# Six transformer layers on one core: the feed-forward statistics, their root and their transposes are put elsewhere in the turn

## The chip, the cores and the metric

The kernel runs on 1 core of one Trainium2 chip. The metric is the device time of one execution in microseconds (us); before the change it is 4221.26 us, the median of 3 runs (4219.84 to 4221.34). All arithmetic is float32, but for a mask of bfloat16.

## The reference, cut to what matters

The input is 8 sequences of 512 tokens with 128 features. The result is the sum of the input, one attention block over the layer-normalised input, and a stack of six layers over the same layer-normalised input. The stack is the part that matters here:

```
for i in range(6):
    x = attn_layer(shift_tokens(x), Wqkv[i], q_scale[i], k_scale[i], Wo[i]) + x
    x = ffn_layer(shift_tokens(x), ln_g[i], ln_b[i], W1[i], b1[i], W2[i], b2[i]) + x
```

- `shift_tokens` moves the upper 64 features one token down.
- `attn_layer`: 16 heads of 64. q and k are divided by their norms over the 64 features of a head, scaled and rotated; each token attends to its own window of 32 tokens and the window before it; softmax, product with v, output product `@ Wo`.
- `ffn_layer`: layer norm over the 128 features (mean, variance, `1/sqrt(var + 1e-5)`), a product with W1 to two halves of 341, `a * gelu(gate)`, a product with W2.

## The kernel before, in words

One stage (0 to about 965 us) does the first attention block; the change does not touch its code, except for one more memset ahead of it. The rest, about 3255 us, is the six layers. It is one software pipeline of **turns**, `layers` (L344) calling `turn(s)` on each engine. A turn is a block of 128 tokens; a batch (one sequence) has four turns, c = 0, 1, 2, 3, and a layer 8 batches, so there are 192 turns. Batches 2 to 6 of a layer run in a hardware loop, where semaphore values are computed from loop registers. Every engine has its own program, in the order in which the code is written, and waits on semaphores for the others. Nothing plans or reorders the work beyond that: the order in `turn` of each engine is the schedule.

In turn t several blocks are in flight at different depths (`s.has(k)`: the block k turns ahead). What each engine does in one turn, in its order, with the line numbers of the profile:

- **VectorE (DVE)**: sums of the exponentials `den` (L956) after ScalarE's exponentials, reciprocal (L958), four rotation products of q and k from PSUM (L909, L911), sums of squares `ss` for the 32 norms of a block (L968), their floor (L970) and the bit-trick guess of the root `rn` (L972); in turn 0 the **feed-forward statistics** of the last batch, `statistics` (bn_stats L918, a memset L921, bn_aggr L923, variance plus eps L926, guess L928); the residual add `x` (L979), the 32x32 transposes of the weights `pT` (L983), in turns 0, 2 and 3 the gate product of the feed-forward (L935), in turn 1 its residual add (L991), row maxima (L1002) and their subtraction (L1005) from the score PSUM, and last `qn`, the product of the rotated q and k with the root (L1012).
- **GpSimd (POOL)**: normalised weights `pn` (L630), two additions that finish the rotations of q (L634) and k (L636), then `newton`, 12 dependent small operations (L399) on 32 columns that refine the root `rn`; in turn 0 after that a second `newton` of 12 on 4 columns (`frn`), and the two products that normalise the tokens of the feed-forward, `fnt` (shown as tile xnT: L645 subtracts the mean, L649 multiplies with the root).
- **TensorE (PE)**: 16 transposes of `qn` (L1053; q to banks 0 and 1, k to banks 4 and 5), the output product (L1265, 32 matmul records into bank 0, over even and then odd heads), feed-forward work (turn 0: up product of chunk 2, L1221; turn 1: 4 transposes of `fnt` to bank 6, L1213, and the down product, L1231; turns 2 and 3: up products of chunks 0 and 1), one transpose of tokens (L1301), scores (L1313, L1318), the product of weights and windows (L1204), which waits for `pT`, and two projections (L1047). In four turns of a layer a `fold` of the next layer's weights stands behind the output product.
- **ScalarE (ACT)**: squares of q (L742), copy of the transposed q to `qT`, both banks in one activation (L746), squares of k (L749), two copies of the transposed k (L754, L755), in turn 1 the copy of the transposed feed-forward tokens (L765), in the others gelu (L734), copy of the transposed tokens (L771), two copies of the product with the windows to `y` (L726), exponentials `es` (L781).
- **SyncE (SP)**: DMA issues; the change moves none of them. The tokens that the statistics read (`xsh`) are loaded at the end of turn 3 (L543 to L545).

The order around the root on DVE before the change, within `turn`:

```
reduce ss -> floor -> guess rn -> [turn 0: statistics, guess frn] -> x += ps_o -> transpose pT -> ...
```

Of the kernel before, what the change touches and what calls it, by code (L numbers as in the profile page):

```python
# [87 lines left out]
def build(nc, x_in, consts, a_logit, a_bout, a_wqk, a_wv, a_wo, l_wqk, l_wv, l_wo, l_scale, l_w1, l_w2, l_small, out, xd, accd, vd):  # L88
# [8 lines left out]
    with ExitStack() as ctx:  # L97
# [43 lines left out]
        ss = sb("ss", [P, 2 * H])  # L141
        c15 = sb("c15", [P, 2 * H])
        root_const = sb("root_const", [P, len(ROOT_CONSTS), 2 * H])
        floor_const = sb("floor_const", [P, 2 * H])
        rn = sb("rn", [P, 2 * H])
        rt = sb("rt", [P, 2 * H])
# [169 lines left out]
        f_gs = sem("f_gs")  # L316
        f_rs = sem("f_rs")
# [234 lines left out]
        def _(pool):  # L552
# [4 lines left out]
            nc.gpsimd.memset(floor_const[:], NORM_FLOOR).then_inc(s_avg, 1)  # L557
            nc.gpsimd.memset(ones, 1.0).then_inc(s_avg, 1)
            pool.wait_ge(s_avg, 3 + len(ROOT_CONSTS))
# [65 lines left out]
            def turn(s):  # L625
                c, t = s.c, s.t
                if s.has(1):
                    pool.wait_ge(l_rd, t + 2)
                    past(pool, l_pT, t + 1)
                    nc.gpsimd.tensor_tensor(heads(pn[:], H), heads(es[:], H),  # L630
                                            rden[:].unsqueeze(2).to_broadcast([P, H, KEYS]), ALU.mult).then_inc(l_p, 1)
                if s.has(3):
                    pool.wait_ge(l_rq, t + 4)
                    nc.gpsimd.tensor_tensor(t1[:, 0:INNER], t1[:, 0:INNER], t2[:, 0:INNER], ALU.add).then_inc(l_rotq, 1)  # L634
                    pool.wait_ge(l_rk, t + 4)
                    nc.gpsimd.tensor_tensor(t1[:, INNER:2 * INNER], t1[:, INNER:2 * INNER], t2[:, INNER:2 * INNER],  # L636
                                            ALU.add).then_inc(l_rotk, 1)
                    pool.wait_ge(l_gs, t + 4)
                    newton(pool, l_rs, t + 3, rn[:], ss[:], rt[:], scaled=True)
                if c == 0 and s.ffn(1):  # L640
                    n = s.f1
                    pool.wait_ge(f_gs, n + 1)
                    newton(pool, f_rs, n, frn[:], fhalf[:], frt[:])
                    past(pool, f_xt, n)
                    nc.gpsimd.tensor_tensor(heads(fnt, NU), xsh[:], agg[:, :, 0:1].to_broadcast([P, NU, DIM]),  # L645
                                            ALU.subtract).then_inc(f_dv, 1)
                    pool.wait_ge(f_dv, n + 1)
                    pool.wait_ge(f_rs, (n + 1) * RS_POOL)
                    nc.gpsimd.tensor_tensor(heads(fnt, NU), heads(fnt, NU), frn[:].unsqueeze(2).to_broadcast([P, NU, DIM]),  # L649
                                            ALU.mult).then_inc(f_xn, 1)  # L650
# [5 lines left out]
        def _(act):  # L656
# [80 lines left out]
            def turn(s):  # L737
# [5 lines left out]
                if s.has(2):  # L743
                    act.wait_ge(l_tq, t + 3)
                    past(act, l_s, t + 2)
                    act.activation(qT[:].rearrange("p h c -> p (h c)"), pool0, ACT.Copy).then_inc(l_qT, 1)  # L746
# [3 lines left out]
                if s.has(2):  # L750
                    if s.turn_of(-1, 2):
                        act.wait_ge(s_zero, 2)
                    act.wait_ge(l_tk, t + 3)
                    act.activation(*keys(0, (c + 2) % NU), ACT.Copy)  # L754
                    act.activation(*keys(1, (c + 2) % NU), ACT.Copy).then_inc(l_kT, 1)  # L755
                part = fold_part(s)
# [6 lines left out]
                if c == 1 and s.ffn(1):  # L763
                    act.wait_ge(f_xt, s.f1 + 1)
                    act.activation(fxn, bank(6), ACT.Copy).then_inc(f_T, 1)  # L765
# [21 lines left out]
        def _(dve):  # L787
# [127 lines left out]
            def statistics(n):  # L915
# [6 lines left out]
                for k in range(NU):  # L922
# [3 lines left out]
                nc.vector.tensor_scalar(fhalf[:], agg[:, :, 1], EPS, 0.5, ALU.add, ALU.mult).then_inc(f_hv, 1)  # L926
                dve.wait_ge(f_hv, n + 1)
                nc.vector.tensor_scalar(frn[:].bitcast(I32), fhalf[:].bitcast(I32), -0.5, float(0x5F3759DF - (1 << 22)),  # L928
                                        ALU.mult, ALU.add).then_inc(f_gs, 1)
# [22 lines left out]
            def turn(s):  # L952
# [8 lines left out]
                if s.has(3):  # L961
                    u = (c + 3) % NU
                    dve.wait_ge(l_sqq, t + 4)
                    past(dve, l_qn, t + 3)
                    rotate(0, u, pool3, l_rq)
                    dve.wait_ge(l_sqk, t + 4)
                    rotate(1, u, pool1, l_rk)
                    nc.vector.tensor_reduce(ss[:], heads(sq[:], 2 * H), X, ALU.add).then_inc(l_ss, 1)  # L968
                    dve.wait_ge(l_ss, t + 4)
                    nc.vector.tensor_tensor(ss[:], ss[:], floor_const[:], ALU.max).then_inc(l_fl, 1)  # L970
                    dve.wait_ge(l_fl, t + 4)
                    nc.vector.tensor_scalar(rn[:].bitcast(I32), ss[:].bitcast(I32), -0.5, float(0x5F3759DF),  # L972
                                            ALU.mult, ALU.add).then_inc(l_gs, 1)
                if c == 0 and s.ffn(1):
                    statistics(s.f1)
                if s.has(0):
                    dve.wait_ge(l_o, t + 1)
                    xb = x[:, bass.ds((s.b * NU + c) * DIM, DIM)]
                    nc.vector.tensor_tensor(xb, xb, ps_o, ALU.add).then_inc(l_x, 1)  # L979
                if s.has(1):  # L980
# [26 lines left out]
                if s.has(3):  # L1007
# [5 lines left out]
                                            rn[:].unsqueeze(2).to_broadcast([P, 2 * H, DH]), ALU.mult).then_inc(l_qn, 1)  # L1013
# [3 lines left out]
            dve.wait_ge(s_avg, 3 + len(ROOT_CONSTS))  # L1017
# [4 lines left out]
        def _(pe):  # L1022
# [28 lines left out]
            def transposes(i, pool, src):  # L1051
                for a in range(PAIRS):
# [156 lines left out]
            def ffn_transpose(n):  # L1209
                pe.wait_ge(f_xn, n + 1)  # L1210
                past(pe, f_h, n * NC)
                for k in range(NU):
                    t = nc.tensor.transpose(bank(6)[:, k * P:(k + 1) * P], fnt[:, k * P:(k + 1) * P], ident)  # L1213
                t.then_inc(f_xt, 1)

# [29 lines left out]
            def turn(s):  # L1245
                c, t = s.c, s.t
                part = fold_part(s)
                if s.has(2):
# [4 lines left out]
                    transposes(0, pool0, qn[:]).then_inc(l_tq, 1)  # L1253
                    past(pe, l_y0sb, t + 1)
                    transposes(1, pool2, qn[:]).then_inc(l_tk, 1)
                if s.has(0):
                    pe.wait_ge(l_y0sb, t + 1)
                    pe.wait_ge(l_y1sb, t + 1)
                    if s.has(2):
                        pe.wait_ge(l_qT, t + 3)  # L1260
                    if s.turn_of(0, 0):
                        pe.wait_ge(s_msb, (s.l + 1) * NU)
                    for odd in range(2):
                        for h in range(odd, H, 2):
                            m = nc.tensor.matmul(ps_o, y[:, h], mhL[s.v][:, slot(h)], start=(h == 0), stop=(h == H - 1))  # L1265
                    m.then_inc(l_o, 1)
                if part is not None:
                    n, v, q = part
                    if s.has(2):
                        pe.wait_ge(l_qT, t + 3)  # L1270
                    past(pe, l_xT, t + 4)
                    fold(n, q)
                if s.turn_of(1, 1):
                    pe.wait_ge(l_qT, t + 3)
# [6 lines left out]
                if c == 1 and s.ffn(1):  # L1281
                    ffn_transpose(s.f1)
# [8 lines left out]
                if s.has(4):  # L1291
                    pe.wait_ge(l_xs[c], (s.l * NB + s.b + 2) * 16)
                    if s.has(2):
                        pe.wait_ge(l_qT, t + 3)
# [4 lines left out]
                    if s.turn_of(1, 1):  # L1299
                        pe.wait_ge(f_bs, s.l + 1)  # L1300
                    nc.tensor.transpose(ps_x[:, 0:P], xs[:, c], ident).then_inc(l_xt, 1)  # L1301
                if s.has(2):
# [6 lines left out]
                    pe.wait_ge(l_qT, t + 3)  # L1309
# [24 lines left out]
                if s.has(4):  # L1334
                    if c == 0 and s.ffn(2):
                        pe.wait_ge(f_h, (s.f2 + 1) * NC)
                    if c == 1 and s.ffn(1):
                        pe.wait_ge(f_T, s.f1 + 1)
# [104 lines left out]
```

## Time and profile before

| what | value |
|---|---|
| median of 3 runs | 4221.26 us (4219.84 to 4221.34) |
| profiled execution, its time | 4222.04 us |
| its span, first to last instruction | 4220.2 us |
| mean granted TensorE clock | 0.990 |
| busy PE, DVE, ACT, POOL | 3945.5, 3868.1, 2606.7, 2696.9 us (93, 92, 62, 64%) |
| turns of the layers | 192, in steady batches 65.09 us for four |

Busy time is an average over the span. Two engines are above 90%, so the shares alone don't say which bounds a turn; the order in time of one steady batch, and what each engine waits for in it, do. In the timeline a row is: start in us from the span's start, duration in us, engine, line, operation, output from inputs, shapes, and in brackets the idle time of that engine ahead of it with what ended it.

### The profile page before, as it was taken

The page shows a single profiled execution, that of the slowest core. Times are in us where ns is not written, and L with a number is a line of the kernel's source. Part 1 is how long each engine was busy: PE and PEld are TensorE (multiplying, and loading weights), DVE is VectorE, ACT ScalarE, POOL GpSimd, SP SyncE. Part 2 cuts the span into 40 slices and gives each one's busy share as a digit, 9 for nine tenths or more (in the row PEclk, how much of TensorE's full clock was granted, in tenths as well). Part 3 has the DMA queues.
Part 4 walks back from the last instruction along what each step waited for, and adds up shares of the span by engine and source line. Part 5 has one row for each costly group of instructions (what it writes and reads, how often), then busy time and mean ns, then how long its engine had stood idle before and what let it go on. Part 6 is the DMA issues. An engine that isn't in the chain of part 4 may idle for free. (4 is left out here: it accounts for less than half of the span.)

```text
span 4220.2 us, 124486 instructions
## 1 busy us (share of the span) xinstructions
PE 3945.5 (93%) x48616; PEld 2740.2 (65%) x48616; DVE 3868.1 (92%) x4452; ACT 2606.7 (62%) x3780; POOL 2696.9 (64%) x4716
## 2 busy tenths in 40 slices
PE   7999999997999999999999999999999999999996
PEld 5666666665666666666666666666666666666664
DVE  5888888887999999999999999999999999999994
ACT  4666666653566666666666665666666666666663
POOL 5565556645667676676667666666676666766663
PEclk9999999999999999999999999999999999999998
DMA  5454554540000011000110001100011000010000
GB/s 136 93 100 95 98 98 92 103 99 20 24 17 15 20 29 29 17 15 17 32 29 16 16 16 31 28 18 15 16 30 30 18 15 16 20 39 18 15 16 14
DMA packets 342439, 165.07 MB, mean 39 GB/s; under 512 B 114240, under 2 KB 337472, under 8 KB 341184
## 3 DMA queue, kind: packets, MB, share of 16 engines
q1 hardware_dynamic: 342208, 161.99, 17.2%
q8 instruction: 145, 2.38, 0.2%
q14 instruction: 86, 0.70, 0.1%
HBM read 115.67 MB, written 33.69 MB: 35 GB/s over the span
## 5 line engine op out<-in xcount | busy, mean ns | idle before, releaser
L630 POOL TENSOR_TENSOR pn<-es,rden 128x1024 f32<-128x1024 f32 x192 | 366.6, 1909 | 695.7 <-DVE rden L958 695.7
L726 ACT ACTIVATE y<-ps 128x1024 f32<-128x1024 f32 x384 | 372.3, 1021 | 503.8 <-PE ps L1204 503.8
L634 POOL TENSOR_TENSOR t<-t 128x1024 f32<-128x1024 f32 x192 | 454.7, 2368 | 69.0 <-DVE t L911 69.0
L678 ACT ACTIVATE t<-ps,amx 128x512 f32<-128x512 f32 x512 | 347.9, 689 | 224.5 <-DVE amx L815 224.5
L909 DVE TENSOR_TENSOR t<-ps,tabl 128x1024 f32<-128x1024 f32 x384 | 467.1, 1216 | 7.8 <-ACT sq L749 4.6
L911 DVE TENSOR_TENSOR t<-ps,tabl 128x1024 f32<-128x1024 f32 x384 | 466.4, 1215 | 0.0
L636 POOL TENSOR_TENSOR t<-t 128x1024 f32<-128x1024 f32 x192 | 453.3, 2361 | 4.7 <-DVE t L911 4.7
L1012 DVE TENSOR_TENSOR qn<-t,rn 128x2048 f32<-128x2048 f32 x192 | 438.1, 2282 | 5.0 <-POOL rn L399 5.0
L968 DVE TENSOR_REDUCE ss<-sq 128x32 f32<-128x2048 f32 x192 | 437.0, 2276 | 0.0
L1053 PEld LDWEIGHTS ps<-cst,qn 128*128 128x128 f32 x3072 | 350.2, 141 | 116.5 <-issue 64.2
L815 DVE TENSOR_REDUCE amx<-ps 128x2 f32<-128x1024 f32 x256 | 311.0, 1215 | 111.3 <-PE ps L1075 111.0
L1265 PE MATMUL ps<-acc,y 128*128 128x128 f32 x3072 | 369.9, 279 | 36.6 <-ACT qT L746 32.3
L1265 PE MATMUL ps<-wm,y 128*128 128x128 f32 x3072 | 365.7, 277 | 33.8 <-ACT qT L746 33.8
L1265 PEld LDWEIGHTS ps<-acc,y 128*128 128x128 f32 x3072 | 354.7, 194 | 57.5 <-issue 57.4
L1265 PEld LDWEIGHTS ps<-wm,y 128*128 128x128 f32 x3072 | 350.2, 192 | 53.9 <-issue 53.9
L1318 PE MATMUL ps<-kpad,qT 128*32 128x128 f32 x12288 | 383.9, 278 | 0.0
L1053 PE MATMUL ps<-cst,qn 128*128 128x128 f32 x3072 | 371.0, 274 | 13.6 <-DVE qn L1012 10.4
L1318 PEld LDWEIGHTS ps<-kpad,qT 128*32 128x32 f32 x12288 | 331.0, 111 | 44.8 <-issue 44.1
L1047 PE MATMUL ps<-wm,xT 128*128 128x512 f32 x768 | 357.5, 608 | 1.4 <-DVE acc L858 0.8
L1047 PE MATMUL ps<-acc,xT 128*128 128x512 f32 x768 | 355.2, 605 | 0.0
L823 DVE STREAM_TRANSPOSE kpad<-t 128x1024 f32<-128x1024 f32 x256 | 315.5, 1232 | 0.0
L1075 PE MATMUL ps<-qk 64*128 64x512 f32 x1024 | 289.6, 643 | 4.3 <-ACT t L678 3.5
(134 smaller groups left out, 8245.4 us busy)
## 6 DMA issues: line engine op xcount, KB each, us to landing
wm<-values_dram SPq DMA_DIRECT2D x128, 256.0 KB, 5.0
y<-values_dram SPq DMA_DIRECT2D x128, 256.0 KB, 4.7
values_dram<-qT SPq DMA_DIRECT2D x64, 256.0 KB, 2.3
tokens_dram<-x SPq DMA_DIRECT2D x96, 128.0 KB
xs<-tokens_dram SPq DMA_DIRECT2D x192, 64.0 KB, 1.8
xw<-tokens_dram SPq DMA_DIRECT2D x192, 64.0 KB, 1.9
xsh<-x SPq DMA_DIRECT2D x48, 128.0 KB
xsh<-x SPq DMA_DIRECT2D x48, 127.0 KB
```

What stands on the lines that cost most here:

```text
L630: nc.gpsimd.tensor_tensor(heads(pn[:], H), heads(es[:], H), rden[:].unsqueeze(2).to_broadcast([P, H, KEYS]), ALU.mult).then_inc(l_p, 1)
L634: nc.gpsimd.tensor_tensor(t1[:, 0:INNER], t1[:, 0:INNER], t2[:, 0:INNER], ALU.add).then_inc(l_rotq, 1)
L636: nc.gpsimd.tensor_tensor(t1[:, INNER:2 * INNER], t1[:, INNER:2 * INNER], t2[:, INNER:2 * INNER], ALU.add).then_inc(l_rotk, 1)
L726: return act.activation(y[:].rearrange("p h (w q) -> p w h q", w=NW)[:, 2 * half:2 * half + 2], src.rearrange("p (w h q) -> p w h q", w=2, ...
L909: nc.vector.tensor_tensor(t13, q3, tabl[:, 0, u, i].unsqueeze(1).to_broadcast([P, H, DH]), ALU.mult)
L911: nc.vector.tensor_tensor(t23.rearrange("p h (s d) -> p h s d", s=2), swapped, tabl[:, 1, u, i].rearrange("p (s d) -> p s d", s=2).unsquee ...
L968: nc.vector.tensor_reduce(ss[:], heads(sq[:], 2 * H), X, ALU.add).then_inc(l_ss, 1)
L1012: nc.vector.tensor_tensor(heads(qn[:], 2 * H), heads(t1, 2 * H), rn[:].unsqueeze(2).to_broadcast([P, 2 * H, DH]), ALU.mult).then_inc(l_qn, 1)
L1047: m = nc.tensor.matmul(pool[:, s * 512:(s + 1) * 512], src, wqkL[v][:, i * INNER + s * 512:i * INNER + (s + 1) * 512], start=True, stop=True)
L1053: t = nc.tensor.transpose(pool[:, a * P:(a + 1) * P], src[:, i * INNER + a * P:i * INNER + (a + 1) * P], ident)
L1265: m = nc.tensor.matmul(ps_o, y[:, h], mhL[s.v][:, slot(h)], start=(h == 0), stop=(h == H - 1))
L1318: m = nc.tensor.matmul(pool1[w * WIN:(w + 1) * WIN, a * 2 * KEYS:(a + 1) * 2 * KEYS], qT[:, a, w * WIN:(w + 1) * WIN], kpad[:, 2 * a:2 * a ...
```

## The change

- The statistics move from turn 0 to turn 1, on DVE ahead of the sums of squares. They no longer make a guess of their own. The variance plus eps goes, times the square of the norms' scale, into 4 new columns of `ss`, now 36 wide; guess, `newton` and the buffers `rn`, `rt`, `root_const` are 36 wide in every turn. `frn`, `fhalf` and `frt` are no longer used here.
- In every turn the residual add `x` stands between the sums of squares and their floor.
- POOL makes `fnt` in turn 1, after the shared `newton`.
- PE transposes `fnt` in turn 2, between the even and the odd heads of the output product, to bank 1 instead of bank 6; ACT copies it there ahead of the gelu. The feed-forward's up product of turn 2 waits for that copy as before.
- The copy of the transposed q is two activations of one bank each, each after its own 4 transposes; the output product waits for the first alone.
- DVE waits in turn 2 for `f_xn` ahead of its guess, since that overwrites the root which POOL's last product reads.

The declarations, the fill of `ss` with ones at the start, and waits whose number alone changes (`l_qT` now counts two a turn) are left out of the diff:

```diff
@@ -635,18 +634,19 @@
                                             ALU.add).then_inc(l_rotk, 1)
-                    pool.wait_ge(l_gs, t + 4)
-                    newton(pool, l_rs, t + 3, rn[:], ss[:], rt[:], scaled=True)
-                if c == 0 and s.ffn(1):
+                roots = t + 4 if s.has(3) else L * NBLK + 1 + (s.static and s.b == NB)
+                if s.has(3) or c == 1 and s.ffn(1):
+                    pool.wait_ge(l_gs, roots)
+                    newton(pool, l_rs, roots - 1, rn[:], ss[:], rt[:], scaled=True)
+                if c == 1 and s.ffn(1):
                     n = s.f1
-                    pool.wait_ge(f_gs, n + 1)
-                    newton(pool, f_rs, n, frn[:], fhalf[:], frt[:])
+                    pool.wait_ge(f_mv, n + 1)
                     past(pool, f_xt, n)
...
                     pool.wait_ge(f_dv, n + 1)
-                    pool.wait_ge(f_rs, (n + 1) * RS_POOL)
-                    nc.gpsimd.tensor_tensor(heads(fnt, NU), heads(fnt, NU), frn[:].unsqueeze(2).to_broadcast([P, NU, DIM]),
+                    pool.wait_ge(l_rs, roots * RS_POOL)
+                    nc.gpsimd.tensor_tensor(heads(fnt, NU), heads(fnt, NU), rn[:, 2 * H:].unsqueeze(2).to_broadcast([P, NU, DIM]),
                                             ALU.mult).then_inc(f_xn, 1)
@@ -741,9 +741,11 @@
                 if s.has(2):
-                    act.wait_ge(l_tq, t + 3)
                     past(act, l_s, t + 2)
-                    act.activation(qT[:].rearrange("p h c -> p (h c)"), pool0, ACT.Copy).then_inc(l_qT, 1)
+                    for half in range(2):
+                        act.wait_ge(l_tq, 2 * t + 5 + half)
+                        act.activation(qT[:, 4 * half:4 * half + 4].rearrange("p h c -> p (h c)"), bank(half),
+                                       ACT.Copy).then_inc(l_qT, 1)
                 if s.has(3):
@@ -753,6 +755,9 @@
                     act.activation(*keys(1, (c + 2) % NU), ACT.Copy).then_inc(l_kT, 1)
+                if c == 2 and s.ffn(1):
+                    act.wait_ge(f_xt, s.f1 + 1)
+                    act.activation(fxn, ps_x, ACT.Copy).then_inc(f_T, 1)
                 part = fold_part(s)
@@ -760,9 +765,6 @@
                     gelu(s.f2, 2, None)
-                if c == 1 and s.ffn(1):
-                    act.wait_ge(f_xt, s.f1 + 1)
-                    act.activation(fxn, bank(6), ACT.Copy).then_inc(f_T, 1)
                 if c >= 2 and s.ffn(1):
@@ -923,10 +925,7 @@
                 dve.wait_ge(f_mv, n + 1)
-                nc.vector.tensor_scalar(fhalf[:], agg[:, :, 1], EPS, 0.5, ALU.add, ALU.mult).then_inc(f_hv, 1)
-                dve.wait_ge(f_hv, n + 1)
-                nc.vector.tensor_scalar(frn[:].bitcast(I32), fhalf[:].bitcast(I32), -0.5, float(0x5F3759DF - (1 << 22)),
-                                        ALU.mult, ALU.add).then_inc(f_gs, 1)
+                nc.vector.tensor_scalar(ss[:, 2 * H:], agg[:, :, 1], EPS, ROOT_SCALE * ROOT_SCALE, ALU.add, ALU.mult).then_inc(f_hv, 1)

@@ -965,18 +964,25 @@
                     rotate(1, u, pool1, l_rk)
-                    nc.vector.tensor_reduce(ss[:], heads(sq[:], 2 * H), X, ALU.add).then_inc(l_ss, 1)
-                    dve.wait_ge(l_ss, t + 4)
-                    nc.vector.tensor_tensor(ss[:], ss[:], floor_const[:], ALU.max).then_inc(l_fl, 1)
-                    dve.wait_ge(l_fl, t + 4)
-                    nc.vector.tensor_scalar(rn[:].bitcast(I32), ss[:].bitcast(I32), -0.5, float(0x5F3759DF),
-                                            ALU.mult, ALU.add).then_inc(l_gs, 1)
-                if c == 0 and s.ffn(1):
+                if c == 1 and s.ffn(1):
                     statistics(s.f1)
+                if s.has(3):
+                    nc.vector.tensor_reduce(ss[:, 0:2 * H], heads(sq[:], 2 * H), X, ALU.add).then_inc(l_ss, 1)
                 if s.has(0):
...
                     nc.vector.tensor_tensor(xb, xb, ps_o, ALU.add).then_inc(l_x, 1)
+                if s.has(3):
+                    dve.wait_ge(l_ss, t + 4)
+                    nc.vector.tensor_tensor(ss[:, 0:2 * H], ss[:, 0:2 * H], floor_const[:], ALU.max).then_inc(l_fl, 1)
+                    dve.wait_ge(l_fl, t + 4)
+                if c == 1 and s.ffn(1):
+                    dve.wait_ge(f_hv, s.f1 + 1)
+                if c == 2 and s.ffn(1):
+                    dve.wait_ge(f_xn, s.f1 + 1)
+                if s.has(3) or c == 1 and s.ffn(1):
+                    nc.vector.tensor_scalar(rn[:].bitcast(I32), ss[:].bitcast(I32), -0.5, float(0x5F3759DF),
+                                            ALU.mult, ALU.add).then_inc(l_gs, 1)
                 if s.has(1):
@@ -1208,10 +1214,16 @@
                 pe.wait_ge(f_xn, n + 1)
-                past(pe, f_h, n * NC)
                 for k in range(NU):
-                    t = nc.tensor.transpose(bank(6)[:, k * P:(k + 1) * P], fnt[:, k * P:(k + 1) * P], ident)
+                    t = nc.tensor.transpose(ps_x[:, k * P:(k + 1) * P], fnt[:, k * P:(k + 1) * P], ident)
                 t.then_inc(f_xt, 1)
+
+            def tokens_transposed(s):
+
+                if s.has(2):
+                    pe.wait_ge(l_qT, 2 * s.t + 6)
+                pe.wait_ge(l_xT, s.t + 4 if s.has(4) else L * NBLK)
+                ffn_transpose(s.f1)

@@ -1250,36 +1262,41 @@
                         past(pe, l_xT, t + 4)
-                    transposes(0, pool0, qn[:]).then_inc(l_tq, 1)
+                    for half in range(2):
+                        transposes(0, pool0, qn[:], half).then_inc(l_tq, 1)
                     past(pe, l_y0sb, t + 1)
...
                     if s.has(2):
-                        pe.wait_ge(l_qT, t + 3)
+                        pe.wait_ge(l_qT, 2 * t + 5)
                     if s.turn_of(0, 0):
...
                     for odd in range(2):
+                        if odd and c == 2 and s.ffn(1):
+                            tokens_transposed(s)
                         for h in range(odd, H, 2):
...
                     m.then_inc(l_o, 1)
+                elif c == 2 and s.ffn(1):
+                    tokens_transposed(s)
                 if part is not None:
                     n, v, q = part
+                    if c == 2 and s.ffn(1):
+                        pe.wait_ge(f_T, s.f1 + 1)
                     if s.has(2):
-                        pe.wait_ge(l_qT, t + 3)
+                        pe.wait_ge(l_qT, 2 * t + 6)
                     past(pe, l_xT, t + 4)
...
                 if s.turn_of(1, 1):
-                    pe.wait_ge(l_qT, t + 3)
+                    pe.wait_ge(l_qT, 2 * t + 6)
                     ffn_bias(s.l)
...
                     ffn_up(s.f2, 2)
-                if c == 1 and s.ffn(1):
-                    ffn_transpose(s.f1)
                 if c == 1 and s.ffn(2):
@@ -1291,13 +1308,15 @@
                     if s.has(2):
-                        pe.wait_ge(l_qT, t + 3)
+                        pe.wait_ge(l_qT, 2 * t + 6)
                     past(pe, l_xT, t + 4)
...
                         pe.wait_ge(f_bs, s.l + 1)
+                    if c == 2 and s.ffn(1):
+                        pe.wait_ge(f_T, s.f1 + 1)
                     nc.tensor.transpose(ps_x[:, 0:P], xs[:, c], ident).then_inc(l_xt, 1)
@@ -1334,8 +1353,6 @@
                         pe.wait_ge(f_h, (s.f2 + 1) * NC)
-                    if c == 1 and s.ffn(1):
-                        pe.wait_ge(f_T, s.f1 + 1)
                     if c == 1 and s.ffn(2):
```

## Rows read from the trace of the kernel before

**Rows 1.** Waits between engines, 1080 to 4190 us: who waited for whom, total us, times, longest

```profile
PE ps L1204 <- DVE pT L983: 68.8, 48, 1.7
PE ps L1265 <- ACT qT L746: 64.3, 183, 0.5
PE ps L1301 <- DVE b1s L947: 14.2, 6, 4.2
...
DVE den L956 <- ACT es L781: 17.9, 89, 2.4
```

**Rows 2.** Timeline of DVE, 2400 to 2475 us: the first operation of five turns

```profile
2404.21 1.22 DVE L956 TENSOR_REDUCE den<-es 128x16 f32<-128x1024 f32 x1
...
2421.53 1.22 DVE L956 TENSOR_REDUCE den<-es 128x16 f32<-128x1024 f32 x1 [0.17 <-ACT es L781]
...
2438.34 1.22 DVE L956 TENSOR_REDUCE den<-es 128x16 f32<-128x1024 f32 x1 [0.16 <-ACT es L781]
...
2453.82 1.22 DVE L956 TENSOR_REDUCE den<-es 128x16 f32<-128x1024 f32 x1
...
2469.31 1.22 DVE L956 TENSOR_REDUCE den<-es 128x16 f32<-128x1024 f32 x1
```

**Rows 3.** Timeline of DVE, the same window: one turn 2 from its sums of squares on

```profile
2444.30 2.27 DVE L968 TENSOR_REDUCE ss<-sq 128x32 f32<-128x2048 f32 x1
2446.61 0.32 DVE L970 TENSOR_TENSOR ss<-ss,floor_const 128x32 f32<-128x32 f32 x1
2446.96 0.18 DVE L972 TENSOR_SCALAR rn<-ss 128x32 int32<-128x32 int32 x1
...
2447.30 1.24 DVE L983 STREAM_TRANSPOSE pT<-pn 128x1024 f32<-128x1024 f32 x1
...
2451.47 2.28 DVE L1012 TENSOR_TENSOR qn<-t,rn 128x2048 f32<-128x2048 f32 x1
```

**Rows 4.** Timelines of PE and of ACT, the same turn 2

```profile
2438.82 1.91 PE L1053 MATMUL ps<-cst,qn 128*128 128x128 f32 x16
...
2448.84 1.14 PE L1204 MATMUL ps<-pT,xw 32*128 32x512 f32 x8
...
2452.73 1.06 ACT L781 ACTIVATE es<-es 128x1024 f32<-128x1024 f32 x1
```

**Rows 5.** Timeline of DVE: the statistics in turn 0, the floor in turn 1

```profile
2412.96 0.87 DVE L918 BATCH_NORM_STATS2 st<-xsh 128x6 f32<-128x128 f32 x4
...
2414.28 0.17 DVE L926 TENSOR_SCALAR fhalf<-agg 128x4 f32<-128x4 f32 x1
2414.49 0.20 DVE L928 TENSOR_SCALAR frn<-fhalf 128x4 int32<-128x4 int32 x1
...
2429.80 1.20 DVE L970 TENSOR_TENSOR ss<-ss,floor_const 128x32 f32<-128x32 f32 x1
```

**Rows 6.** Timeline of POOL, 2400 to 2475 us

```profile
2414.42 0.24 POOL L399 TENSOR_TENSOR rt<-rn 128x32 f32<-128x32 f32 x1
...
2419.16 2.25 POOL L399 TENSOR_TENSOR frt<-frn 128x4 f32<-128x4 f32 x1
...
2422.21 1.05 POOL L645 TENSOR_TENSOR xnT<-xsh,agg 128x512 f32<-128x512 f32 x1
...
2428.59 2.36 POOL L636 TENSOR_TENSOR t<-t 128x1024 f32<-128x1024 f32 x1
...
2444.52 2.36 POOL L636 TENSOR_TENSOR t<-t 128x1024 f32<-128x1024 f32 x1
...
2450.83 0.25 POOL L399 TENSOR_TENSOR rn<-rn,rt 128x32 f32<-128x32 f32 x1
```

**Rows 7.** Timelines of PE and of ACT: the feed-forward tokens in turn 1

```profile
2427.83 0.60 PE L1213 MATMUL ps<-cst,xnT 128*128 128x128 f32 x4
...
2428.47 0.60 ACT L765 ACTIVATE qk<-ps 128x512 f32<-128x512 f32 x1 [1.58 <-PE ps L1213]
```

**Rows 8.** Timeline of the end of the span, PE

```profile
4196.88 4.56 PE L1231 MATMUL ps<-w,fh 128*128 128x128 f32 x24
```

More of the change, by code:

```diff
@@ L140, in build @@
         msel = sb("msel", [P, 2, P], BF16)
-        ss = sb("ss", [P, 2 * H])
+        ss = sb("ss", [P, 2 * H + NU])
         c15 = sb("c15", [P, 2 * H])
-        root_const = sb("root_const", [P, len(ROOT_CONSTS), 2 * H])
+        root_const = sb("root_const", [P, len(ROOT_CONSTS), 2 * H + NU])
         floor_const = sb("floor_const", [P, 2 * H])
-        rn = sb("rn", [P, 2 * H])
-        rt = sb("rt", [P, 2 * H])
+        rn = sb("rn", [P, 2 * H + NU])
+        rt = sb("rt", [P, 2 * H + NU])
         mx = sb("mx", [P, H])
@@ L315, in build @@
         f_hv = sem("f_hv")
-        f_gs = sem("f_gs")
-        f_rs = sem("f_rs")
         f_dv = sem("f_dv")
@@ L557, in _ @@
             nc.gpsimd.memset(floor_const[:], NORM_FLOOR).then_inc(s_avg, 1)
+            nc.gpsimd.memset(ss[:], 1.0).then_inc(s_avg, 1)
             nc.gpsimd.memset(ones, 1.0).then_inc(s_avg, 1)
-            pool.wait_ge(s_avg, 3 + len(ROOT_CONSTS))
+            pool.wait_ge(s_avg, 4 + len(ROOT_CONSTS))
             def token_root(b):
@@ L1012, in turn @@
                     nc.vector.tensor_tensor(heads(qn[:], 2 * H), heads(t1, 2 * H),
-                                            rn[:].unsqueeze(2).to_broadcast([P, 2 * H, DH]), ALU.mult).then_inc(l_qn, 1)
+                                            rn[:, 0:2 * H].unsqueeze(2).to_broadcast([P, 2 * H, DH]), ALU.mult).then_inc(l_qn, 1)
             dve.wait_ge(s_tb, 16)
             scale_tables(0)
-            dve.wait_ge(s_avg, 3 + len(ROOT_CONSTS))
+            dve.wait_ge(s_avg, 4 + len(ROOT_CONSTS))
             layers(dve, turn)
@@ L1049, in project, with transposes @@
                 return m
-            def transposes(i, pool, src):
-                for a in range(PAIRS):
+            def transposes(i, pool, src, half=None):
+                for a in range(PAIRS) if half is None else range(half * 4, half * 4 + 4):
                     t = nc.tensor.transpose(pool[:, a * P:(a + 1) * P], src[:, i * INNER + a * P:i * INNER + (a + 1) * P], ident)
@@ L1308, in turn @@
                         past(pe, l_sub, t + 2)
-                    pe.wait_ge(l_qT, t + 3)
+                    pe.wait_ge(l_qT, 2 * t + 6)
                     pe.wait_ge(l_kT, t + 3)
```

## The prediction

> **What bounds the kernel now.** The page gives PE and DVE over 90% busy, which does not say who waits for whom, so I read the waits first. PE waits for `pT` once a batch (48 times, 1.4 us each) and for the copy `qT` in nearly every turn (0.35 us each); DVE waits a little for the exponentials before `den` [rows 1]. Next, the starts of `den` give the length of each turn of a steady batch: 17.32 (turn 0), 16.81, 15.48, 15.49, together 65.10 us [rows 2]. Then I follow turn 2 on all engines. From `den` (2438.34) DVE works without a gap to the end of `pT` (2447.30 + 1.24 = 2448.54): 10.20 us [rows 2, 3]. PE starts the product with the windows 0.30 later, ScalarE copies `y` and ends `es` at 2453.79, and the next `den` starts at 2453.82 [rows 2, 4]. So there is a **ring** den, pT, windows, y, es, den of 10.20 + 5.28 = 15.48 us. PE's own order takes the same 15.48: from its transposes (2438.82) to the windows are 10.02 us, of which about 0.35 are the wait for `qT` [rows 1, 4]. In turns 2 and 3 the ring and PE are tied. In turn 0 the ring is longer by the statistics (PE waits 1.4 us at L1204), in turn 1 PE is (down product and transposes).
>
> A second thing matters: POOL and DVE block each other. In turn 2 POOL's addition L636 ends at 2446.88 and DVE's floor L970 at 2446.93; in turn 1 they end at 2430.95 and 2431.00, and there L970, a matter of 32 columns, shows 1.20 us [rows 3, 5, 6]. The other way round, a POOL operation on 4 columns that meets `qn` takes 2.25 us instead of 0.20 [rows 6]. DVE operations with both inputs in SBUF and POOL's exclude each other, and the later one waits to the other's end.
>
> **Part 1, the add before the floor (all turns).** From guess to `pT` are 0.34 us, of which the add `x` fills 0.21. The floor cannot end before POOL's addition anyway, so the add falls into that wait: the reduction's end is 2446.57, the add takes it to about 2446.8, the floor still ends at 2446.93 [rows 3, 6]. Gain on the ring between 0 (the add pushes the floor) and 0.21; I take 0.15, since waits for two semaphores now stand bare between guess and `pT`. `newton` has slack: from the guess to its last result are 4.12 us for 32 columns (2446.96 to 2451.08) and, at 1.6 ns a column and operation from the 32- and 4-column rows, 4.2 for 36. DVE needs it 4.51 - 0.21 = 4.3 us after the guess [rows 3, 6].
>
> **Part 2, the copy by banks (all turns).** PE's wait of 0.35 goes: the first 4 transposes end some 0.5 us into the 1.9, a 512-column copy takes 0.60 [rows 7], both before the k transposes end. PE's turn becomes about 15.13, the ring stays the longer one. Worth nothing by itself, but it lets Part 1 show, and pays for Part 4. It costs ScalarE some 0.1 a turn, hidden by its waits for PE.
>
> **Part 3, the statistics.** *Turn 0* loses them (1.74 with the guess [rows 5]) and follows the ring: 15.48 - 0.15 = 15.33, a gain of 1.99. POOL's own 12 small steps, the blocked one (2.25) and L645, L649 also leave turn 0, so POOL is no longer late in turn 1 and the floor is not held 0.9 us there.
> *Turn 1*, counted from `den`. The reduction used to start at 5.96 (2444.30 - 2438.34); the statistics now start there and their last operation, the `tensor_scalar` of the variance, is issued 1.32 us later, at 7.28 [rows 2, 3, 5]. POOL's L636 runs until 8.54. Does it hold that operation? At the low end it does not (reduction at 7.4); at the high end all the statistics queue behind POOL (reduction near 10.0), which their rows speak against: four bn_stats took 0.87 with POOL's small steps beside them. The nearest row is L928, also a 4-column `tensor_scalar`: 0.20 us, ending at 2414.69, 0.03 after a POOL step (2414.42 + 0.24) [rows 5, 6]. That is the pattern of L970, so I take it as held: it ends at 8.6, the reduction starts at 8.5. Then reduction, add, floor (now free of POOL) 2.7 us: guess at 11.2, `pT` from 11.33 to 12.57. By the ring the next `den` would come at 12.57 + 5.28 = 17.85. But POOL goes from `newton` (ends 11.2 + 4.2 = 15.4) without a wait into L645, 1.05 us, which reads SBUF, and DVE reaches `qn` at about 15.5: it is held until 16.45, ends near 18.6, and `den` starts at 18.55. PE is not the bound there (its 16.81 fall by 0.35 and by the transposes); it will wait for `pT` in turn 1 instead of turn 0. Turn 1: +1.74.
>
> The Trainium skill, page "SBUF — State Buffer", section "Who interferes with whom", says that a `tensor_scalar` between SBUF tensors can enter a mode with two ports and is then blocked for the whole of a GpSimd instruction, and bn_stats is not among those it names. Row L928 alone would allow a delay of 0.03 us; by the page it would be the rest of L636. The sum by the page is the one above, the sum without it is rival A.
>
> **Part 4, tokens in turn 2.** PE does the 4 transposes (0.60 alone, about 0.45 in a stream) there: PE's turn 15.13 + 0.45 = 15.6 from transposes to transposes, but after the late `qn` PE starts nearer to `den` (0.3 instead of 0.48), so 15.42 from `den` to `den`. POOL's L649 runs after `qn`, ready 1.1 us after it; PE needs it 3.7 us into its turn. ScalarE's copy (0.60) comes after its k copies, about 5.2 us into the turn, and the up product needs it at 6.0. Cost 0.09 over the ring. If the copy came 1 us later, PE would wait for it. DVE's new wait for `f_xn` was met long ago. Turn 3: 15.33. No DMA is moved.
>
> **The sum.** 15.33 + 18.55 + 15.42 + 15.33 = 64.63 against 65.10: -0.47 a batch, 48 batches: -22.6. In the six batches with the bias (PE already waits 2.4 us for DVE's `b1s` [rows 1]) turn 1 takes the 1.2 us of later statistics in full, and turn 0, which has a fold, had no 2 us to win: +1.1 each, +6.6 (estimate). At the end the down product (4.56 us [rows 8]) no longer stands between the last statistics and the last up products, the copy (0.6) and the wider root (0.6) come in: -3.3. Together -19.3 from the profiled execution, 4222.0: 4202.7. That execution is 0.8 above the median of the runs shown, well inside what I can tell. Forecast **4203 us**.
>
> **Rivals.**
> A. *The variance operation is not held by POOL.* Then in turn 1 guess at 10.1, `den` at 17.45: 63.53 a batch, -75 + 6.6 - 3.3: **4150 us**. For: L926 itself always shows 0.17 next to POOL's steps, and it reads with a step; against: it fell into a gap between two of them (2414.35 to 2414.42), and L928.
> B. *The add only pushes the floor, or the bare waits cost what it gave.* Ring 15.48, turn 2 15.55: 65.06 a batch, with the corrections **4223 us**. No change.
> C. *Slower: PE stays the bound.* The two copies, each with its fixed part and its semaphore, reach PE no earlier than one did. Then turns 0 and 3 stay 15.48, turn 2 carries the transposes (15.93), turn 1 18.55: 65.44, +16 + 3: **4241 us**. It decides from 0.35 us on, a second copy's worth. Against: the output product needs the first copy alone, and that can be done 0.6 us before the last transpose.
> D. The high end of Part 3, all statistics behind L636: turn 1 +1.4 more, **4270 us**.
>
> **Chances.** Forecast 0.57 (own range 4188 to 4217), A 0.22 (4138 to 4168), B 0.11, C 0.07, D 0.03. What a measurement of this kernel tells from no change is about 0.2%, 8 us: faster takes most of the forecast's case and all of A, 0.70; same 0.20 (B and the forecast's upper edge); slower 0.10. The range 4148 to 4226 holds the forecast, B and two thirds of A, about 0.82.
>
> **What would show it.** Turn 0 near 15.3 between two `den`, turn 1 between 17.4 and 18.6, the rest just under 15.4. PE's wait for `qT` at L1265 gone; its wait for `pT` in turn 1, about 1 us. L926 at 1.2 us instead of 0.17: the forecast; still 0.17: A. L1012 in turn 1 at about 3.2 us instead of 2.28; if it stays 2.28 in that turn the hold by L645 is wrong, and turn 1 is shorter by 0.7. `den` to `pT` unchanged in turns 2 and 3: B. L1265 starting 2.25 us after L1053 as before: C.

## The result and the profile after

The changed kernel takes 4186.18 us, the median of 4 runs (4179.85 to 4188.69), against 4220.83 us for the kernel before (4219.84 to 4221.34): ratio 0.9914, 95% interval 0.9899 to 0.993. So it is 34.7 us faster. The forecast was 4203 us, 18 us faster: right in sign, and the time lies in the range (4148 to 4226), but the kernel gained nearly twice what was forecast. The profiled execution took 4187.27 us.

The page of the changed kernel: span, then busy us and share by engine.

```profile
span 4185.5 us, 124350 instructions
...
PE 3931.9 (94%) x48616; PEld 2739.3 (65%) x48616; DVE 3844.2 (92%) x4406; ACT 2616.1 (63%) x3972; POOL 2586.2 (62%) x4165
```

The waits of PE and DVE from 1080 to 4150 us (us in total, times, longest), which answer to [rows 1]:

```profile
PE ps L1210 <- DVE pT L989: 87.1, 77, 3.5
PE ps L1320 <- DVE b1s L946: 26.4, 6, 6.2
PE ps L1059 <- DVE qn L1018: 16.2, 38, 3.2
...
DVE den L955 <- ACT es L783: 15.1, 65, 2.4
```

The wait for `qT` (64.3 us) is gone. PE now waits for `pT` and, 38 times, for `qn`: DVE has taken the lead. The wait for the bias has grown by 12 us in its six turns. Next the starts of `den` on DVE's timeline, from turn 3 of one batch to the end of turn 2 of the next, against [rows 2]:

```profile
2373.80 1.21 DVE L955 TENSOR_REDUCE den<-es 128x16 f32<-128x1024 f32 x1
...
2388.89 1.21 DVE L955 TENSOR_REDUCE den<-es 128x16 f32<-128x1024 f32 x1
...
2404.24 1.22 DVE L955 TENSOR_REDUCE den<-es 128x16 f32<-128x1024 f32 x1 [0.17 <-ACT es L783]
...
2422.59 1.21 DVE L955 TENSOR_REDUCE den<-es 128x16 f32<-128x1024 f32 x1
...
2437.67 1.21 DVE L955 TENSOR_REDUCE den<-es 128x16 f32<-128x1024 f32 x1
```

| turn | before | forecast | after |
|---|---|---|---|
| 0 | 17.32 | 15.33 | 15.35 |
| 1 | 16.81 | 18.55 | 18.35 |
| 2 | 15.48 | 15.42 | 15.08 |
| 3 | 15.49 | 15.33 | 15.09 |
| batch | 65.10 | 64.63 | 63.87 |

Turns 0 and 1 came out within 0.2 us of the forecast: turn 0 became 2.0 us shorter and turn 1 1.5 us longer. Of the miss of 0.76 us a batch, turns 2 and 3 hold 0.58 and turn 1 the rest. DVE's timeline of turn 1 and of the end of the next turn, against [rows 3, 5]:

```profile
2410.20 0.86 DVE L920 BATCH_NORM_STATS2 st<-xsh 128x6 f32<-128x128 f32 x4
...
2411.52 1.29 DVE L928 TENSOR_SCALAR ss<-agg 128x4 f32<-128x4 f32 x1
2412.72 2.27 DVE L970 TENSOR_REDUCE ss<-sq 128x32 f32<-128x2048 f32 x1
...
2415.32 0.18 DVE L984 TENSOR_SCALAR rn<-ss 128x36 int32<-128x36 int32 x1
2415.41 1.24 DVE L989 STREAM_TRANSPOSE pT<-pn 128x1024 f32<-128x1024 f32 x1
...
2419.55 3.12 DVE L1018 TENSOR_TENSOR qn<-t,rn 128x2048 f32<-128x2048 f32 x1
...
2430.93 0.24 DVE L977 TENSOR_TENSOR ss<-ss,floor_const 128x32 f32<-128x32 f32 x1
2431.20 0.18 DVE L984 TENSOR_SCALAR rn<-ss 128x36 int32<-128x36 int32 x1
2431.30 1.24 DVE L989 STREAM_TRANSPOSE pT<-pn 128x1024 f32<-128x1024 f32 x1
```

and POOL's beside it, against [rows 6]:

```profile
2410.42 2.36 POOL L635 TENSOR_TENSOR t<-t 128x1024 f32<-128x1024 f32 x1
...
2419.48 1.04 POOL L645 TENSOR_TENSOR xnT<-xsh,agg 128x512 f32<-128x512 f32 x1
2420.68 2.88 POOL L649 TENSOR_TENSOR xnT<-xnT,rn 128x512 f32<-128x512 f32 x1 [0.16 <-POOL xnT L645]
```

Both holds of the forecast are there. The `tensor_scalar` on 4 columns takes 1.29 us and ends at 2412.81, 0.03 after POOL's addition (2410.42 + 2.36 = 2412.78). `qn` takes 3.12 us, since L645 ran until 2420.52; and L649 in turn waits behind `qn` (2.88 us, against 1.04 before the change). Last PE's timeline, against [rows 4, 7]:

```profile
2399.19 1.14 PE L1210 MATMUL ps<-pT,xw 32*128 32x512 f32 x8 [0.32 <-DVE pT L989]
...
2416.78 1.14 PE L1210 MATMUL ps<-pT,xw 32*128 32x512 f32 x8 [1.65 <-DVE pT L989]
...
2422.73 1.96 PE L1059 MATMUL ps<-cst,qn 128*128 128x128 f32 x16 [0.31 <-DVE qn L1018]
2424.53 1.95 PE L1280 MATMUL ps<-wm,y 128*128 128x128 f32 x16
2426.31 0.60 PE L1218 MATMUL ps<-cst,xnT 128*128 128x128 f32 x4
2426.75 1.95 PE L1280 MATMUL ps<-wm,y 128*128 128x128 f32 x16
...
2432.67 1.14 PE L1210 MATMUL ps<-pT,xw 32*128 32x512 f32 x8
```

In turn 1 the windows start 0.13 us after `pT` (2415.41 + 1.24), although PE had stood idle, and so they do in turn 2. That is the ring's own delay there. The 0.30 between them in turn 2 of the kernel before was PE arriving. In turn 0 (the first row) the delay is 0.33 us with PE idle, in the loop's batches before and after the change alike; the cause of the difference between the turns was not tried.

### The profile page after: what moved, and what is told of

It is laid out like the page before. It is cut to its first block, busy times and chain, and to the rows that moved or that the text cites. A ratio compares the mean times of both kernels' runs of the same rounds, so it can differ in the third digit from the quotient of the medians.

```text
span 4185.5 us, 124350 instructions
## 1 busy us (share of the span) xinstructions
PE 3931.9 (94%) x48616; PEld 2739.3 (65%) x48616; DVE 3844.2 (92%) x4406; ACT 2616.1 (63%) x3972; POOL 2586.2 (62%) x4165
## 4 chain that ended last, share of the span: by engine, by line
PE 52%; DVE 25%; issue 11%; POOL 7%; ACT 4%; POOLq 0%; DMA 0%; DVEq 0%; ACTq 0%; SPq 0%
PE ps L1280 10%; PE ps L1210 7%; PE ps L1053 6%; PE ps L1337 5%; PE ps L1059 5%; PE ps L1233 5%; DVE t L911 4%; DVE qn L1018 3%; DVE t L913 3%; PE ps L1116 3%; DVE kpad L825 3%; DVE den L955 2%; POOL rt L397 2%; ACT y L726 2%; PE ps L1081 2%
## 5 line engine op out<-in xcount | busy, mean ns | idle before, releaser
L1018 DVE TENSOR_TENSOR qn<-t,rn 128x2048 f32<-128x2048 f32 x192 | 468.9, 2442 | 6.1 <-POOL rn L397 6.1
L1210 PE MATMUL ps<-pT,xw 32*128 32x512 f32 x1536 | 222.3, 648 | 95.9 <-DVE pT L989 92.0
```

What stands on the lines that cost most here:

```text
L1018: nc.vector.tensor_tensor(heads(qn[:], 2 * H), heads(t1, 2 * H), rn[:, 0:2 * H].unsqueeze(2).to_broadcast([P, 2 * H, DH]), ALU.mult).then_ ...
L1210: m = nc.tensor.matmul(pools[w // 2][:, w % 2 * 512:(w % 2 + 1) * 512], (xs if new else xw)[rows, u], pT[rows, new].rearrange("p h q -> p ...
```

## The experiments

Theory S: before the change PE alone held turns 2 and 3 at 15.48. The ring, with 0.13 in place of 0.30, was 15.31, and DVE's own order about 15.33, both just behind it. Theory R is the forecast's: the ring was 15.48 too. The change moves the statistics (the move), puts the residual add ahead of the floor (the add) and copies the transposed q by banks (the split). Kernels marked "on before" carry only the parts named; the others alter the changed kernel. "Batch" is the sum of four steady turns; in e1, e4 and e8 some batches differ, as said there. Differences in the total are between medians.

| kernel | median us | ratio to before, 95% | turns 0, 1, 2, 3 | batch |
|---|---|---|---|---|
| e1_split_alone (on before) | 4207.11 | 0.9963 (0.9951 to 0.9976) | 17.32, 16.24, 15.34, 15.33 | 64.2 |
| e2_add_alone (on before) | 4210.04 | 0.9971 (0.9961 to 0.9982) | 17.0, 16.8, 15.48, 15.48 | 64.8 |
| e8_split_and_add (on before) | 4198.07 | 0.9938 (0.9922 to 0.9955) | 18.0, 16.9, 15.1, 15.1 | 65.1 |
| e9_move_alone | 4248.06 | 1.0059 (1.0042 to 1.0076) | 15.7, 18.3, 15.6, 15.5 | 65.1 |
| e3_one_copy | 4245.44 | 1.0054 (1.0037 to 1.0071) | 15.62, 18.37, 15.62, 15.48 | 65.1 |
| e4_add_late | 4215.49 | 0.9985 (0.9975 to 0.9994) | 15.68, 18.29, 15.33, 15.33 to 15.46 | 64.6 to 64.75 |
| e5_variance_late | 4122.05 | 0.9762 (0.9746 to 0.9779) | 15.36, 17.10, 15.10, 15.1 | 62.7 |
| e6_mean_early | 4171.09 | 0.9876 (0.986 to 0.9893) | 15.35, 17.55, 15.34, 15.1 | 63.3 |
| e7_both | 4103.09 | 0.9719 (0.9703 to 0.9735) | 15.37, 16.28, 15.33, 15.1 | 62.1 |

**e1, the copy by banks alone.**

```diff
-                    transposes(0, pool0, qn[:]).then_inc(l_tq, 1)
+                    for half in range(2):
+                        transposes(0, pool0, qn[:], half).then_inc(l_tq, 1)
...
-                    act.activation(qT[:].rearrange("p h c -> p (h c)"), pool0, ACT.Copy).then_inc(l_qT, 1)
+                    for half in range(2):
+                        act.wait_ge(l_tq, 2 * t + 5 + half)
+                        act.activation(qT[:, 4 * half:4 * half + 4].rearrange("p h c -> p (h c)"), bank(half),
+                                       ACT.Copy).then_inc(l_qT, 1)
```

> The kernel before with the copy of the transposed q by banks, nothing else. Theory S (in turns 2 and 3 of the kernel before PE alone was the bound at 15.48 us, the ring over pT, windows and es had some 0.17 us of slack since pT to windows needs 0.13 us and not the 0.30 that stood there, and DVE's own order is 15.33): turns 2 and 3 fall to 15.33, turn 1 from 16.81 to about 16.5, turn 0 stays 17.3; -0.6 us a batch, about -30 us. Theory R (that of the prediction: the ring was 15.48 too): turns 0, 2 and 3 unchanged, turn 1 -0.35, about -16 us.

Measured: 15.34 and 15.33 in turns 2 and 3, as theory S had it to 0.01; R is out. DVE's timeline of one batch:

```profile
2328.18 1.21 DVE L958 TENSOR_REDUCE den<-es 128x16 f32<-128x1024 f32 x1
...
2345.50 1.22 DVE L958 TENSOR_REDUCE den<-es 128x16 f32<-128x1024 f32 x1 [0.17 <-ACT es L783]
...
2361.74 1.22 DVE L958 TENSOR_REDUCE den<-es 128x16 f32<-128x1024 f32 x1
...
2377.08 1.21 DVE L958 TENSOR_REDUCE den<-es 128x16 f32<-128x1024 f32 x1
...
2392.41 1.21 DVE L958 TENSOR_REDUCE den<-es 128x16 f32<-128x1024 f32 x1
```

The total, -15 us, missed the -30 expected. The steady batch gained 0.87, but in some ten batches turn 0 was about 1.6 us longer, and in the last layer a batch gained only 0.13. PE's row in a turn 0 of the longer kind:

```profile
3401.31 1.93 PE L1206 MATMUL ps<-pT,xw 32*128 32x512 f32 x8 [2.29 <-DVE pT L985]
```

After an idle time of 2.29 us the eight matmuls took 1.93 us and not 1.14. A PE that comes to L1206 earlier waits longer there (1.62 us before the change), and in those batches it runs slower after the wait.

**e2, the add alone.** `x += ps_o` moved from behind the guess to ahead of the floor, on the kernel before.

> The kernel before with the residual add moved ahead of the floor, nothing else. Theory S and theory R alike: PE holds turns 1, 2 and 3 at 16.81 and 15.48, so only turn 0, which PE does not hold, falls, by 0.2 to 0.25: -10 us. If instead DVE or the ring held turns 2 and 3, they fall by 0.25 each: -30 us or more.

Measured: -12 us; turn 0 -0.3, turns 1, 2 and 3 unchanged. With PE holding them, DVE's saving does not show.

**e8, both of these.** The edits of e1 and e2 together.

> The kernel before with both the copy of the transposed q by banks and the residual add ahead of the floor; the statistics, their root and their transposes stay where they were. Theory S (PE and DVE each stood just behind the other, so the two savings are worth more together than apart): turns 2 and 3 at 15.09 (apart: 15.33 and 15.48), turn 1 at 16.24, turn 0 at 17.0, together 63.4 us a batch against 65.1 before and 63.9 in the changed kernel; -1.7 a batch, about -65 us less 10 to 20 for turns in which TensorE's clock falls after its wait in turn 0: 4155 to 4175, faster than the changed kernel, whose move of the statistics then cost time. Rival (the two only add up): -15 - 12 = -27, about 4195 us, turns 2 and 3 at 15.33; the move of the statistics then gained.

Turns 2 and 3 fell to 15.1, as S had it: the two savings together give what neither gives alone. The total did not follow: -24 us, where S had -47 to -67. Turn 0 was not 17.0 but about 18.0 (17.6 to 18.7), and turn 1 mostly longer than its 16.24. PE's timeline in turn 0:

```profile
2407.05 1.55 PE L1207 MATMUL ps<-pT,xw 32*128 32x512 f32 x8 [1.97 <-DVE pT L986]
2408.35 1.96 PE L1207 MATMUL ps<-pT,xs 32*128 32x512 f32 x8
```

Three stretches around it: us, busy us of PE, PEld, DVE, ACT and POOL, and as the last three columns granted clock, DMA share and GB/s:

```profile
2395.00:2407.00 12.00, 10.08 (x121) 7.85 (x119) 11.82 (x24) 8.48 (x12) 8.88 (x13) 1.00 0.06 16
2407.00:2413.00 6.00, 5.95 (x22) 2.38 (x23) 4.90 (x4) 2.57 (x3) 4.98 (x15) 0.72 0.08 22
2413.00:2419.00 6.00, 6.00 (x48) 5.23 (x47) 5.62 (x6) 5.13 (x7) 5.79 (x5) 1.00 0.00 0
```

The granted clock is 1.00 before and after and 0.72 in the 6 us after the wait: part of them at 1.2 instead of 2.4 GHz. The second group of matmuls takes 1.96 us instead of 1.04. Most steady batches are 1.7 us longer in this way (65.1 against 63.4 us). S had allowed 10 to 20 us for it; it is far more.

**e9, the move alone.** The edits of e3 and e4 together.

> The changed kernel with one copy of the transposed q and the residual add behind the guess: what is left of the change is the move of the statistics, their shared root and the token transposes in turn 2. Theory S: PE holds turns 2 and 3 (15.62 and 15.48 as with one copy), turn 0 near 15.7, turn 1 at 18.3: 65.1 to 65.3 us a batch against 65.1 before, so the move alone gains nothing and with the longer bias turns costs 20 to 30 us: about 4245 us. Rival (the move is worth by itself the difference between the changed kernel and the one with copy and add alone, 12 us): about 4210 us.

Measured: +24 us, as S expected. Its steady batches take 65.1 us as before; the 24 us lie in the batches around the ends of the layers and in the last layer. So the move by itself costs 24 us; on top of split and add it gains some 11 (-35 against -24). The steady batches suggest why: the batches of e8 in which the clock held took 63.4 us, less than the 63.87 of the changed kernel, but most took 65.1. In the changed kernel PE's long wait stands in turn 1 (1.65 us), and the steady batch shown above (2373.8 to 2437.7) runs at a granted clock of 1.00 throughout.

**e3, one copy in the changed kernel.**

```diff
-                    for half in range(2):
-                        act.wait_ge(l_tq, 2 * t + 5 + half)
-                        act.activation(qT[:, 4 * half:4 * half + 4].rearrange("p h c -> p (h c)"), bank(half),
-                                       ACT.Copy).then_inc(l_qT, 1)
+                    act.wait_ge(l_tq, 2 * t + 6)
+                    act.activation(qT[:].rearrange("p h c -> p (h c)"), pool0, ACT.Copy).then_inc(l_qT, 2)
```

> The changed kernel with the transposed q copied by one activation of both banks. PE gets back its wait for qT (0.5 us a turn by the row after, 0.35 by the row before). Theory S: PE is the bound again, turn 3 at 15.48, turn 2 at 15.9 with its token transposes, turn 0 about 15.5, turn 1 unchanged at 18.36: +1.3 us a batch, +55 to +60 us. Rival (DVE alone holds the changed kernel and has room for a slower PE): under +15 us.

Measured: +59 us against the changed kernel. Turn 3 is back at 15.48, turn 2 at 15.62 (S said 15.9: PE enters that turn closer to `den`, since `qn` is late). The forecast gave the split "nothing by itself"; taking it out costs more than the whole gain of 35.

**e4, the add late in the changed kernel.** The residual add back behind the guess.

> The changed kernel with the residual add back behind the guess of the root. Theory S: DVE's own order holds turns 2 and 3 of the changed kernel, so each gets the 0.25 us back, turn 0 0.2, turn 1 about 0.1 (no POOL operation holds its floor): +0.75 us a batch, +35 us. By the size in the prediction (0.15 a turn): +20 us. Rival (PE holds them at 15.09): under +10 us.

Measured: +29 us. Turn 0 +0.33, turn 1 -0.07, turn 2 +0.25, turn 3 +0.24 and in two of the layers +0.36. In the other turns POOL's addition holds the floor anyway and hides the add; in turn 1 nothing holds it, so nothing is hidden.

**e5, the variance late.** It takes away the overlap, not the operation.

```diff
                 stat.then_inc(f_mv, 1)
-                dve.wait_ge(f_mv, n + 1)
-                nc.vector.tensor_scalar(ss[:, 2 * H:], agg[:, :, 1], EPS, ROOT_SCALE * ROOT_SCALE, ALU.add, ALU.mult).then_inc(f_hv, 1)
...
                     nc.vector.tensor_tensor(xb, xb, ps_o, ALU.add).then_inc(l_x, 1)
+                if c == 1 and s.ffn(1):
+                    dve.wait_ge(f_mv, s.f1 + 1)
+                    nc.vector.tensor_scalar(ss[:, 2 * H:], agg[:, :, 1], EPS, ROOT_SCALE * ROOT_SCALE, ALU.add, ALU.mult).then_inc(f_hv, 1)
```

> The changed kernel with the tensor_scalar of the variance behind the residual add of turn 1, where POOL is idle, instead of ahead of the sums of squares, where POOL's second addition runs. Theory H (POOL's addition holds it): it takes 0.17 us instead of 1.29, turn 1 falls from 18.36 to about 17.3, -1.1 us a batch, -45 to -50 us, about 4138. Rival (the 1.29 us belong to the operation, or the statistics as such are slow there): it shows 1.29 in the new place too and the time does not change.

Measured: -64 us against the changed kernel, 4122 us. Turn 1 is 17.10, 1.25 shorter. DVE's timeline:

```profile
2320.64 0.16 DVE L975 TENSOR_SCALAR ss<-agg 128x4 f32<-128x4 f32 x1
...
2325.19 3.12 DVE L1019 TENSOR_TENSOR qn<-t,rn 128x2048 f32<-128x2048 f32 x1
```

The operation takes 0.16 us, and `qn` is still held. The -45 to -50 us expected were missed: turn 1 gained 1.25 and not 1.1, in nearly every batch, and 8 of the 64 us lie outside the turns (3.4 behind the last `den`, 4.8 ahead of the first, where nothing was changed). Rival A of the prediction described this kernel, and its turn 1 (17.45) was 0.35 too long.

**e6, the mean early.** POOL's subtraction L645 ahead of the shared `newton`.

```diff
+                if c == 1 and s.ffn(1):
+                    pool.wait_ge(f_mv, n + 1)
+                    past(pool, f_xt, n)
+                    nc.gpsimd.tensor_tensor(heads(fnt, NU), xsh[:], agg[:, :, 0:1].to_broadcast([P, NU, DIM]),
+                                            ALU.subtract).then_inc(f_dv, 1)
                 roots = t + 4 if s.has(3) else L * NBLK + 1 + (s.static and s.b == NB)
```

> The changed kernel with POOL's subtraction of the mean ahead of the shared root, in the 2.8 us in which POOL waits for the guess in turn 1. Theory H: qn in turn 1 takes 2.28 us instead of 3.12 and the turn falls from 18.36 to about 17.55 (the ring over pT then binds), -0.8 us a batch, about -35 us. Rival (qn of turn 1 is late for another reason, or the earlier subtraction holds the floor instead): no change, or the floor of turn 1 at about 1 us.

POOL's and DVE's timelines:

```profile
2345.18 1.04 POOL L641 TENSOR_TENSOR xnT<-xsh,agg 128x512 f32<-128x512 f32 x1
```

```profile
2352.02 2.29 DVE L1020 TENSOR_TENSOR qn<-t,rn 128x2048 f32<-128x2048 f32 x1
...
2354.22 1.21 DVE L957 TENSOR_REDUCE den<-es 128x16 f32<-128x1024 f32 x1
...
2369.56 1.22 DVE L957 TENSOR_REDUCE den<-es 128x16 f32<-128x1024 f32 x1 [0.15 <-ACT es L785]
```

The hold is gone and turn 1 is 17.55, as expected, but the total gained 15 us and not 35. Turn 2 rose by 0.25 to 15.34 (PE starts its transposes 0.47 us after `den` and not 0.14, so the 4 token transposes show there), and the gain is missing in the last layer and in the turns with the bias.

**e7, both moves.**

> Both moves of the two kernels before this one. If the two holds are separate and in series on DVE: turn 1 falls from 18.36 to about 16.5, -1.9 us a batch, -80 to -85 us, about 4103 us. If they overlap (the ring over pT binds once one is gone), no more than -55.

Measured: 4103.09 us, as expected to the microsecond, and faster than both kernels: 0.9719 of before. Turn 1 is 16.28, so the two holds are separate and in series; turn 2 is 15.33 as in e6.

## Why the prediction was right or wrong

- **The ring and PE tied at 15.48**: this step failed. It read the 0.30 us between `pT` and the windows in turn 2 as the ring's own delay; it is 0.13. The ring was 15.31, and only PE stood at 15.48 (e1, e2). A row in which two chains end together does not tell which of them set the time. Another turn can: in the last layer of the kernel before, turn 2 is 15.32 us long, with 0.13 from `pT` to the windows. DVE's and PE's timelines there:

```profile
3901.79 1.21 DVE L956 TENSOR_REDUCE den<-es 128x16 f32<-128x1024 f32 x1
...
3910.74 1.24 DVE L983 STREAM_TRANSPOSE pT<-pn 128x1024 f32<-128x1024 f32 x1
...
3917.11 1.21 DVE L956 TENSOR_REDUCE den<-es 128x16 f32<-128x1024 f32 x1
```

```profile
3912.11 1.14 PE L1204 MATMUL ps<-pT,xw 32*128 32x512 f32 x8
```

Turn 0, where PE waited 1.62 us, would have misled: the delay there is 0.33. So a delay is best read in a turn of the same kind, and e1 decides. In the changed kernel the ring (15.31 - 0.25 = 15.06) and DVE's own order (15.09) again lie too close to tell apart; no run parts them.
- **Part 1, 0.15 taken between 0 and 0.21**: mis-sized. `den` to the start of `pT` in turn 2 fell from 8.96 (2447.30 - 2438.34) to 8.71 (2431.30 - 2422.59), 0.25 us. The floor still ends 0.05 us after POOL's addition; from the guess to `pT` are 0.10 us instead of 0.34, so no bare wait appeared.
- **Part 2, PE 0.35**: mis-sized. The wait alone is 0.35, but from the start of the transposes to the product were 2.25 us and are 1.75 in turn 1 (2404.65 to 2406.40) and 1.80 in turn 2 of the changed kernel, 0.45 to 0.50 less. And "worth nothing by itself" was wrong: e1.
- **Turn 0** (-1.99 forecast, -1.97): right as to what leaves the turn, but the exact hit is luck. By e4 turn 0 without the add is 15.68 and not 15.48, and the add is worth 0.33 there and not 0.15; the two errors cancel.
- **Turn 1** (+1.74, +1.54): right, with both of its holds (e5, e6, e7). The hold of the `tensor_scalar` was chosen from one row with a delay of 0.03 us; the operation took 1.12 us longer, and e5 shows that it is POOL's overlap. The trace agrees with the page that the prediction names (the Trainium skill, "SBUF — State Buffer", section "Who interferes with whom"): 1.29 us for the `tensor_scalar`, and no delay for bn_stats (0.86 us for four beside POOL's addition).
- **Turn 2** (-0.06, -0.40) and **turn 3** (-0.16, -0.40): the consequence of the first three points. 0.6 us a batch over some 36 steady batches is 21 us, more than the whole miss of 17; turn 1 adds 7, and the next point took back a part.
- **The bias turns, the ends of the layers and the end** did worse than forecast. Steady batches became 1.2 us shorter; the six with the bias together became 1.7 longer, which is 9 us more than six steady ones give, against 6.6 forecast. Five batches at the ends of layers, whose turn 1 takes 21.4 to 22.2 us instead of 19.5 to 19.6, cost another 6 us, which the forecast did not have. From the last `den` to the end the profiled executions took 57.7 us before and 60.3 after, against -3.3 forecast. The down product no longer stands between the transposes and the up products; the three up products behind the transposes are slower instead:

PE's timeline near the end of the changed kernel:

```profile
4162.06 3.78 PE L1233 MATMUL ps<-qk,w1s 128*128 128x512 f32 x4 [0.69 <-ACT qk L760]
```

and the stretch around it, with the columns of the stretches above:

```profile
4160.00:4176.00 16.00, 11.62 (x16) 3.95 (x16) 1.50 (x2) 1.97 (x3) 0.14 (x1) 0.50 0.00 1
```

At a granted clock of 0.50, its lower level, the three up products take 3.68 to 3.78 us each; in the kernel before they took 1.92 to 1.96. All kernels with the move show this: in e3 to e7 and e9 two of the three take 3.4 to 3.8 us and the end takes 56.7 to 57.2. None of the kernels without it does (before, e1, e2, e8: 1.96 at most, and 56.3 to 57.7 for the end). There the down product, 24 matmuls in 4.5 to 5.0 us, runs ahead of them. That its work is what raised the clock in time is the likely reading; no run tests it alone. The time to the first `den` also varies, from 996.8 to 1003.2 us, though the runs do not differ in what that stage does.

- **Rival C** (PE stays the bound) was half true: PE was the bound, and the split removed it. Its price for a split that gives PE nothing, 4241 us, is near e3 and e9, which have no split: 4245 and 4248.

## What to carry to other kernels

When two engines are both nearly full, read each chain's length in a like turn where the other has slack before calling them tied, and try the two savings together: in turns 2 and 3 e1 gains 0.15 us, e2 nothing, and both together 0.4. Ask of each POOL operation which DVE operation it can meet, however small: 4 columns cost 1.1 us because of their place, and moving two operations within their own engines (e7) was worth 83 us, over twice the change itself. A saving on TensorE that only lengthens its wait can be followed by a lower clock (e8: 0.72 in the 6 us after it).

## What the runs showed of the hardware

- A `tensor_scalar` from SBUF to SBUF on 4 columns, with a step of two on its input, waited for the end of a GpSimd `tensor_tensor` on 128x1024 that was under way: 1.29 us beside it, 0.16 with GpSimd idle (e5). A memset (0.06 us) and four bn_stats (0.86 us, 0.87 before) beside the same GpSimd operation were not delayed.
- TensorE's granted clock dropped after an idle time as short as 2 us within otherwise full work. After 1.97 us (e8) it was 0.72 in the next 6 us and matmuls ran for a while at about half pace (1.96 against 1.04 us); after 2.29 us (e1) eight matmuls took 1.93 us instead of 1.14. After 1.65 us in turn 1 of the changed kernel, and after 3.31 us in one of its longer turns 1, it stayed at 1.00. After 2.29 us it happened in about ten batches and not in the others. What decides was not tried.
- From the end of `pT` to the first matmul on it, with PE idle, were 0.33 us in turn 0 and 0.13 in turn 1 of the same loop, and 0.06 in the first turns of the stage. What makes the difference was not tried.
